# A transformer layer with a sparse-column FFN: the FFN's columns moved three groups behind the attention's front, and a new order of the prologue

## What is computed

```python
xn = layernorm(x)                                  # no gain or bias
x = x + attention(xn) + ffn(xn)

# attention: 16 heads of 16, rotary q and k, a bias by bucket of distance, causal softmax, output projection
# ffn, for each token:
similarity = l2norm(xn) @ l2norm(col_emb).T        # 16 columns
gate_values = sigmoid(gelu(xn @ gate_w1 + gate_b1) @ gate_w2 + gate_b2)
logits = similarity + gate_values
mask = one_hot(argmax(logits)); weights = mask * softmax(logits)
cols = gelu(einsum('bsd,cdn->bscn', xn, W_cols) + b_cols) * weights[..., None]   # 16 columns x 64 neurons
y = cols.reshape(B, S, -1) @ proj_w + proj_b + xn
out = (y - mean(y)) * rsqrt(var(y) + 1e-5) * ln_g + ln_b
```

## Time and profile before

| | us |
|---|---|
| three runs, median (lowest to highest) | 2100.35 (2096.41 to 2103.63) |
| the profiled execution | 2098.83 |
| its span, first to last instruction | 2097.0 |
| PE, DVE, ACT, POOL busy | 1872.3, 1595.2, 1104.2, 631.1 |

### The profile page before, as it was taken

How to read it: one execution, slowest core, us unless ns; L and a number is a source line. 1 busy time by engine, 2 the same in 40 slices (tenths; PEclk the granted TensorE clock), 3 DMA queues, 4 the chain that set the end, 5 groups by cost and what they waited for, 6 DMA issues and landing times.

```text
span 2097.0 us, 40927 instructions
## 1 busy us (share of the span) xinstructions
PE 1872.3 (89%) x10854; PEld 1023.3 (49%) x10854; DVE 1595.2 (76%) x5475; ACT 1104.2 (53%) x2142; POOL 631.1 (30%) x848
## 2 busy tenths in 40 slices
PE   4887899999999999999999999999999999997776
PEld 2654455555445555455555554455545554453223
DVE  2235788888888788887888788887887788877883
ACT  2232455555665455565555556655555556554444
POOL 4463332233333223333333133333222333300000
PEclk9989999999999999999999999999999999998988
DMA  8413122233212222232122332122222321122101
...
DMA packets 199392, 144.67 MB, mean 69 GB/s; under 512 B 60428, under 2 KB 186780, under 8 KB 199149
## 3 DMA queue, kind: packets, MB, share of 16 engines
...
## 4 chain that ended last, share of the span: by engine, by line
PE 58%; DVE 14%; issue 12%; POOL 6%; ACT 4%; SPq 4%; DMA 1%; DVEq 0%; ACTq 0%; POOLq 0%
PE scores L1079 12%; PE rows L1023 9%; PE o_bank L1007 9%; PE scores L990 7%; PE bank L1090 7%; PE bank L1036 5%; DVE rows L1172 3%; DVE scores L1151 3%; PE bank L1108 3%; ACT probs L876 3%; PE scores L1081 3%; DVE maxima L1177 2%; SPq L601 2%; POOL rot L795 1%; POOL qk L788 1%
## 5 line engine op out<-in xcount | busy, mean ns | idle before, releaser
L876 ACT ACTIVATE probs<-scores 128x512 f32<-128x512 f32 (+1 forms) x1280 | 670.4, 555 | 497.5 <-DVE scores L1151 251.2
L1177 DVE TENSOR_REDUCE maxima<-rows 128x1 f32<-128x384 f32 (+4 forms) x896 | 473.8, 551 | 120.6 <-PE rows L1023 118.5
L990 PE MATMUL scores<-stack_q,stack_k 99*128 99x512 bf16 (+3 forms) x1536 | 432.9, 337 | 96.6 <-ACT probs L876 67.8
L1023 PE MATMUL rows<-stack_k,stack_q 96*128 96x256 bf16 (+3 forms) x2048 | 460.0, 292 | 44.2 <-issue 14.8
L1172 DVE CUSTOM_DVE_ANT_0 rows<-rows,near_rows 128x256 f32<-128x256 f32 (+1 forms) x1024 | 395.2, 431 | 87.3 <-PE rows L1023 85.3
L1151 DVE TENSOR_TENSOR scores<-scores,near_cols 128x256 f32<-128x256 f32 x768 | 323.2, 433 | 68.0 <-PE scores L990 66.4
L1023 PEld LDWEIGHTS rows<-stack_k,stack_q 96*128 96x128 bf16 x2048 | 170.8, 98 | 408.8 <-issue 146.7
L1007 PE MATMUL o_bank<-probs,v_aug 128*32 128x512 f32 (+3 forms) x3072 | 322.8, 508 | 6.1 <-ACT probs L876 6.1
L1079 PE MATMUL scores<-xn_t,w_cols 128*128 128x256 f32 x1024 | 288.1, 405 | 3.1 <-ACT others_t L922 3.1
L1090 PE MATMUL bank<-w_proj,act_t 128*128 128x256 f32 x1024 | 259.2, 389 | 11.4 <-DVE y L1207 9.7
L990 PEld LDWEIGHTS scores<-stack_q,stack_k 99*128 99x128 bf16 x1536 | 144.7, 99 | 227.9 <-ACT probs L876 146.4
...
## 6 DMA issues: line engine op xcount, KB each, us to landing
...
```

The source lines that it names most:

```text
L876: act.activation(probs[:, (g * NS + s) % PROBS, h, 0:width], ring[(rings + ring_n[1]) % RING][:, 0:width], ACT.Exp, scale=float(D) ** -0.5 ...
L990: ins = pe.matmul(ring[(rings + ring_n[1]) % RING][:, c0:c0 + w], stack_k[g % 2][:, h, kb * P:(kb + 1) * P], stack_q[g % 2][:, h, q0:q0 + ...
L1023: ins = pe.matmul(tile[:, at:at + k1 - k0], stack_q[ag % 2][0:STACK, h, qb * P:(qb + 1) * P], stack_k[ag % 2][0:STACK, h, k0:k1], start=Tr ...
L1177: ins = dve.tensor_reduce(maxima[:, part, m:m + n], tile[:, at:at + n * w].rearrange("p (n w) -> p n w", w=w), AX.X, ALU.max)
```

## The change

The FFN of a chunk moves three groups later. Group G still does the front of chunk G + 5, but the neurons of chunk G + 2 and the columns of chunk G + 1. As xn and xn_t do not live that long, they are kept in one tile (`kept`), written to DRAM at `x_turn`, and read back into another (`again`, whose halves are `skip` and `ffn_t`) at the new stage `ffn_in`, at score slot 8. The first chunk writes into `again` directly. `weight` and `others_t` get a place for each of four chunks. `rest` is made from a second load of x at the new stage `rest_in` (slot 24), and stored at the new stage `keep_rest` (slot 19); x of the chunk after next is loaded at `x_turn` in place of `mask_turn`. The load of v becomes a stage of its own, `load_v`.

The prologue is no longer one chunk after the other: BETWEEN holds the second half of one front and the first half of the next. Two chunks get neurons, one gets columns. The stack halves of groups 0 and 1 are loaded as soon as two chunks are through, the 12 early row tiles stand beside the fronts of chunks 3 and 4, the 28 late ones in the last plan. POOL's rotary writes its first two products into `rot` in place of `swapped`. The near tables are loaded after the parts of the second chunk and no longer after the first chunk's v.

```diff
@@ -129,16 +129,18 @@
           6: [('columns', 7)],
           7: [('x_turn', None)],
           9: [('y2_stats', None)],
+          8: [('ffn_in', None)],
           10: [('skip', None)],
           11: [('qk_begun', 0), ('qk', 0)],
           12: [('load_q', None), ('v', 0)],
           15: [('finish', None), ('qk_begun', 1)],
           16: [('qk', 1)],
           17: [('hidden', None)],
-          19: [('v', 1)],
+          19: [('keep_rest', None), ('v', 1)],
           21: [('gate', None), ('o_turn', 0)],
           23: [('qk_turn', 0), ('choose', None)],
           25: [('left', 0), ('tie', None), ('middle', 0)],
+          24: [('rest_in', None)],
...
-ALONE = ([("stats", None), ("center", None), ("x_turn", None)] + [("columns", k) for k in range(C_PIECES)]
-         + [("qk_begun", 0), ("qk", 0), ("qk_begun", 1), ("qk", 1), ("y2_stats", None), ("skip", None),
-            ("hidden", None), ("v", 0), ("gate", None), ("v", 1), ("choose", None), ("qk_turn", 0),
-            ("left", 0), ("tie", None), ("choice", None), ("finish", None), ("middle", 0), ("qk_turn", 1),
-            ("left", 1), ("mask_turn", None)]
-         + [("neurons", (k, m)) for k in range(2) for m in range(N_PIECES)] + [("middle", 1)]
-         + [("neurons", (k, m)) for k in range(2, 4) for m in range(N_PIECES)])
-CLOSING = [("load", None), ("neurons", (0, 0)), ("neurons", (0, 1)), ("pv", NS - 1), ("o_out", 1),
+NEURONS = [("neurons", (k, m)) for k in range(EM // N_PIECES) for m in range(N_PIECES)]
+
+
+FIRST = ["stats", "center", "x_turn", "qk_begun 0", "qk 0", "qk_begun 1", "qk 1", "v 0", "v 1", "hidden", "gate"]
+BETWEEN = ["next center", "choose", "next x_turn", "qk_turn 0", "left 0", "middle 0", "later stats", "tie",
+           "next qk_begun 0", "next qk 0", "qk_turn 1", "left 1", "choice", "middle 1", "next qk_begun 1", "next qk 1",
+           "mask_turn", "next v 0", "next v 1", "next hidden", "next gate"]
+FINAL = [stage for stage in BETWEEN if stage.split()[0] not in ("next", "later")]
+CLOSING = [("load", None), ("load_v", None), ("neurons", (0, 0)), ("neurons", (0, 1)), ("pv", NS - 1), ("o_out", 1),
            ("neurons", (1, 0)), ("neurons", (1, 1)), ("neurons", (2, 0)), ("shift", None),
            ("neurons", (2, 1)), ("neurons", (3, 0)), ("neurons", (3, 1)), ("o_turn", 1), ("shift_turn", None)]
 FRONT = {"stats", "center", "x_turn", "qk_begun", "qk", "v", "hidden", "gate", "choose", "tie", "choice",
-         "qk_turn", "mask_turn", "left", "middle", "neurons", "skip"}
-FRONT_LATER = {"columns", "y2_stats", "finish"}
+         "qk_turn", "mask_turn", "left", "middle"}
+FFN = {"ffn_in", "skip", "rest_in", "neurons"}
+FFN_LATER = {"columns", "y2_stats", "finish", "keep_rest"}
...
@@ -232,7 +236,8 @@
     o = Order()
     for g in range(NG):
         has_front = batch + (g + LEAD) // NC < B
-        has_later = batch + (g + LEAD - 1) // NC < B
+        has_ffn = batch + (g + 2) // NC < B
+        has_later = batch + (g + 1) // NC < B
         has_next = not (batch == B - 1 and g == NG - 1)
         has_load = batch < B - 1 or g + 2 < NG
...
-    for g in range(-LEAD, 0):
-        plan = [p for p in ALONE if p[0] in FRONT or g > -LEAD]
-        if g == -1:
-
-            o.add("load_q", -2)
-            o.add("load_k", -2)
-            o.add("load", -2)
-            plan = with_rows(plan, len(plan) // 5, len(plan) - 1, ALL_ROWS)
-        for stage, arg in plan:
-            o.add(stage, g, arg)
-    o.add("widen", -1)
-    o.add("load_q", -1)
-    o.add("load_k", -1)
-    o.add("load", -1)
+
+    def add(stage, g):
+        stage, *arg = stage.removeprefix("next ").removeprefix("later ").split()
+        o.add(stage, g, int(arg[0]) if arg else None)
+
+    def between(g, beside):
+        for stage in BETWEEN:
+            at = g + {"next": 1, "later": 2}.get(stage.split()[0], 0)
+            if at < 0:
+                add(stage, at)
+            for stage, at, arg in beside.get(stage, []):
+                o.add(stage, at, arg)
+
+    for stage in FIRST:
+        add(stage, -LEAD)
+        if stage == "x_turn":
+            o.add("stats", -4)
+    between(-5, {})
+    between(-4, {"middle 1": [("load_q", -2, None), ("load_k", -2, None)],
+                 "next hidden": [("skip", -2, None)]})
+    pieces = [[(stage, -2, arg) for stage, arg in NEURONS[k:k + N_PIECES]] for k in range(0, len(NEURONS), N_PIECES)]
+    between(-3, {**dict(zip(("next x_turn", "next qk 0", "next qk 1", "next v 1"), pieces)),
+                 "middle 1": [("load_q", -1, None), ("load_k", -1, None)], "next gate": [("rest_in", -2, None)]})
+    early = len(EARLY) * GH
+    rows = [[("row", -1, row) for row in ALL_ROWS[k:k + 2]] for k in range(0, early, 2)]
+    between(-2, {**dict(zip(("choose", "left 0", "middle 0", "next qk 1", "next v 1", "next gate"), rows)),
+                 "middle 1": [("load", -2, None), ("load_v", -2, None)]})
+    plan = [(stage, int(arg[0]) if arg else None) for stage, *arg in map(str.split, FINAL)]
+    plan += [("y2_stats", None), ("ffn_in", None), ("load", None), ("widen", None), ("finish", None)]
+    plan += [("skip", None), ("load_v", None), ("keep_rest", None), ("rest_in", None)] + NEURONS
+    for stage, arg in [("columns", k) for k in range(C_PIECES)]:
+        o.add(stage, -1, arg)
+    done = early
+    for at, (stage, arg) in enumerate(plan):
+        o.add(stage, -1, arg)
+        upto = early + (len(ALL_ROWS) - early) * (at + 1) // len(plan)
+        for row in ALL_ROWS[done:upto]:
+            o.add("row", -1, row)
+        done = upto
     o.add("shift", -1)
     o.add("shift_turn", -1)
...
-        skip = sb("skip", [P, CT, C])
+        kept = sb("kept", [P, 2, CT * C])
+        xn = kept[:, 0, :].rearrange("p (t f) -> p t f", f=C)
+        xn_t = kept[:, 1, :].rearrange("p (k n) -> p k n", n=CH)
+        again = sb("again", [P, 2, CT * C])
+        skip = again[:, 0, :].rearrange("p (t f) -> p t f", f=C)
+        ffn_t = again[:, 1, :].rearrange("p (k n) -> p k n", n=CH)
+
+        def normed(g):
+
+            return (skip, ffn_t) if g == -LEAD else (xn, xn_t)
+
         rest = sb("rest", [P, CT, C])
         qk = sb("qk", [P, CT, 2 * C])
-        swapped = sb("swapped", [P, 2 * C])
         rot = sb("rot", [P, CT, 2 * C])
         parts = [sb(f"part{i}", [P, 2 * KC, CH], BF16) for i in range(3)]
         left = sb("left", [P, 2 * KC, P])
...
 
+        def ffn_of(b, g, ahead):
+
+            m = g + ahead
+            if g < 0:
+                return m // NC, m % NC, m
+            fb, c = b + m // NC, m % NC
+            return fb, c, fb * NC + c
+
         def next_group(b, g):
 
             ab, ag = (0, 0) if g < 0 else (b, g + 1) if g + 1 < NG else (b + 1, 0)
...
+
+                    elif stage == "load_v":
+                        tb, tg, ti = loaded_group(b, g)
+                        sp.wait_ge(v_out, (tb + 1) * (NC * 16))
+                        alone(sp)
 
                         wait(sp, v_aug_ready, ti)
                         alone(sp)
@@ -647,11 +692,11 @@
                         sp.wait_ge(v_ready, n * CT + CT)
                         alone(sp)
                         sp.dma_start(v_d[fb, :, c * CT:(c + 1) * CT, :], v[:, :, :]).then_inc(v_out, 16)
+                    elif stage == "x_turn":
                         if g > -LEAD:
-                            store_rest(fb, c, n)
-                        else:
-                            load_near()
-                    elif stage == "mask_turn":
+                            sp.wait_ge(bank_drained[i], use + 2)
+                            alone(sp)
+                            sp.dma_start(kept_d[fb, c], kept[:, :, :]).then_inc(kept_out, 16)
                         if not isinstance(n, int) or n + 2 < B * NC:
                             load_x(*((fb, c + 2) if c + 2 < NC else (fb + 1, c + 2 - NC)))
                     elif stage == "middle" and arg == 1:
@@ -660,8 +705,26 @@
                             alone(sp)
                             sp.dma_start(parts_d[fb, i, :, :, c * CH:(c + 1) * CH].rearrange("q p t -> p q t"),
                                          parts[i][:, :, :]).then_inc(parts_out[i], 16)
-                    elif stage == "finish" and isinstance(n, int) and n == B * NC:
-                        store_rest(fb, c, n)
+                        if g == 1 - LEAD:
+                            load_near()
+                    elif stage == "ffn_in":
+                        mb, mc, m = ffn_of(b, g, 2)
+                        sp.wait_ge(kept_out, m * 16)
+                        alone(sp)
+
+                        wait(sp, moments2_ready, m)
+                        alone(sp)
+                        sp.dma_start(again[:, :, :], kept_d[mb, mc]).then_inc(kept_in, 16)
+                    elif stage == "rest_in":
+                        mb, mc, m = ffn_of(b, g, 2)
+                        wait(sp, rest_out, m * 16)
+                        alone(sp)
```

(37 more changed lines are left out.)

99 lines of the change are left out of this document (52 added, 47 removed).

## The result

| | before | after |
|---|---|---|
| median, us, of the executions (their number; lowest to highest) | 2099.88 of 4 (2096.41 to 2103.63) | 2069.53 of 4 (2062.47 to 2077.07) |
| ratio, 95% interval | | 0.9852 [0.9818, 0.9886] |
| profiled execution / its span, us | 2098.83 / 2097.0 | 2062.47 / 2060.7 |
| first shift transfer issued, us | 220.8 | 167.3 |
| groups 0 to 26, us | 1628.8 | 1629.0 |

The changed kernel is faster by 1.5%, 30 us between the medians; 49 were forecast. The last three lines cut each span at SP's issues of the shift transfers, as the prediction did. The profiled execution is the fastest of the four of after, so its 36.3 us less of span is the favourable end: 53.5 us from the prologue, 3.2 from group 0 (62.0 to 58.8), 3.4 lost in groups 1 to 26, 17.0 lost in the last five.

A forecast was written before the change was run, and what follows sets the result against it. Middle groups were taken as bound by PE, the last groups by no full engine, with 224.5 us before the first score. 2098.8 - 56 (prologue) + 0 (middle) + 8 (last groups) = 2050.8, said as 2050; 8-in-10 range 2024 to 2082.

The forecast's parts named there:

- Prologue, -56: Start to first score: 168.4 us against 224.5 before, bounds 155 (-69) and 185 (-39).
- round 0: Prologue: DVE stops until the third chunk's x arrives at 53.5 us, then POOL goes on, ending at 65.
- Round 3: Prologue: POOL first held by `rest_in`'s x, then 13.5 us of POOL or 17 of DVE; end at 120, bounds 112 and 126.
- The second halves: Prologue: group 0's second stack halves landed after chunk 3's parts, taken as 128 us, from 115 to 131.
- x at 53.5: Prologue, round 0: third chunk's x, issued at about 30 us behind sheared bias writes that land at 52.7.
- Step 8: Prologue's end: shift, turn, copy 2.3 us plus 3.6 to first score, 5.9; group 1's 12 loads no longer in the way.
- bound by its chains: Prologue rival: interleaving brings little beyond the FFN that left; first score at 185 to 195, 2067 to 2077 us; 17%.
- rule against interleaving: Prologue: second engine blocked until the first's instruction ends; 7.8 us a chunk in place of 2.4, 27 us longer, 2077.
- The clock: Prologue rival: lower clock slows PE's fronts; rounds 0 and 1 together 10 us more, 2060; counted inside the forecast, no own chance.
- Middle groups, 0 with bounds of -3 and +10: 27 middle groups: reload shifts POOL 3 us inside 7 us of slack, so cost 0, bounds -3 and +10 us.
- Last groups, +8: Groups 27 to 30: 52 us of moved PE work mostly fills 47 us of idle; +8 us, bounds 0 and +20.
- give all back: Last groups rival: 52 us of PE work unhidden, 2095 us, no measurable change; 7%.

The follow-up runs named there:

- b1_x_first: Third chunk's x issued ahead of the sheared bias writes, else as the changed kernel: median 2058.15 us, ratio 0.9807 to the kernel before, first shift at 159.6.
- a2_late: Changed kernel with early stack halves and early row tiles undone, fronts still interleaved: median 2069.4 us, 0.9852 of the kernel before, first shift at 169.3.
- a3_serial_late: Changed kernel with interleaving, early stack halves and early row tiles undone: median 2079.32 us, 0.9914 of the kernel before, first shift at 180.8.
- b3_both: Changed kernel with third chunk's x ahead of the sheared writes and first `rest_in` two chunks sooner: median 2057.37 us, 0.9789 of the kernel before.
- c2_tail: Changed kernel with most FFN matmuls left out of the last groups, other work kept: median 2055.85 us, 0.9801 of before; groups 27-31 255.7 us.

## Why the prediction was right or wrong

The sign and the size of the larger term were right, the size of the smaller was not: 2050 was forecast and 2069.5 measured, inside the range, 3.5 us above the forecast's own span of 2038 to 2066; the profiled execution, 2062.5, lies inside that too.

- **Prologue, -56: right.** First score at 171.5 (168.4 forecast, 224.5 before): -53. *The steps:* round 0 with x at 54.4 (53.5) and its end at 66.6 (65); round 1's rotary at 82.9 (81); round 2 at 102.4 (103). *Round 3* was the one mis-sized: it ended at 127.1 instead of 120, above its bound of 126, since `rest_in` held POOL not a few us but 10.6. The second halves let the first late tile go at 134.8 (128 forecast), and the late tiles ended at 165.2, after 30.4 us instead of 34.5, so part of it came back.
- **A step that was right by its number and thin in its reason**: x at 53.5. I took it as queued behind the sheared writes' landing; the timeline has SP itself spending 12.2 us on the issue, and b1_x_first shows that place alone is worth 8 us.
- **Step 8, no row of loads ahead of the shift: true, and worth at most 1.7 us**, since a2_late undoes the early tiles with it. I gave the absence of the loads no term of its own, but counted it among what shortens the end. a2_late has the row back, and it is hidden. What shortened the end was that 20.2 us of FFN a chunk were gone: -40 of -53.5 is there in a3_serial_late.
- **Rival "bound by its chains"** (first score at 185 to 195): wrong in size, since interleaving bought 10 to 11.5 us. But chains there are: two late x alone cost 12.6 us (167.6 to 155.0 in b3_both).
- **The rule against interleaving** (the Trainium skill, "SBUF — State Buffer", "Who interferes with whom"): the trace agrees with it, and my reading of the 0.61 us as a price in its place was wrong. Three of DVE's rows, and POOL's beside the first two:

```profile
680.46 1.27 POOL L859 TENSOR_TENSOR qk<-qk,rotary 128x512 f32<-128x512 f32 x1
680.54 1.24 DVE L1327 SCALAR_TENSOR_TENSOR logits<-gate_th,like 128x32 f32<-128x32 f32 x1
...
1044.34 1.27 POOL L859 TENSOR_TENSOR qk<-qk,rotary 128x512 f32<-128x512 f32 x1
1044.96 0.69 DVE L1327 SCALAR_TENSOR_TENSOR logits<-gate_th,like 128x32 f32<-128x32 f32 x1
...
1047.26 0.18 DVE L1334 TENSOR_TENSOR tied<-logits,top 128x32 f32<-128x32 f32 x1
```

DVE's operation ends 0.05 us after POOL's instruction (at 1.24 us where it began 0.08 us behind its start, at 0.69 where 0.62 behind), and so do, within 0.01 us, all 49 of `logits`, `tied`, `below`, `ranked` and `others` that took over 0.24 us in before and after. What is paid is the rest of POOL's instruction. `left`, which has one of its two inputs in PSUM, took 0.68 to 0.69 us in all 64 cases in after, beside POOL or not. The price stayed low because few of them met one: before the first shift 8 of 25 did in after, for 4.0 us in all, where I had 2.4 a chunk and the rule at its full price 7.8; one chunk after the other it had been 15 of 25, for 7.8 us in all. Rounds 1 and 2 ended within 2 us of a sum without it.
- **The clock** in the rounds: it fell as feared, 0.63 in 54 to 65, and 0.78 in the last plan, which I had at full clock; both are inside the times above.
- **Middle groups, 0 with bounds of -3 and +10: inside them, some 5 us worse.** The slack after the reload is 3.3 us where I had 7 less 3, and the second wait of POOL, for the x of `rest_in`, is 1.9 us in the quoted group. Both are hidden. What isn't hidden is the clock's stretches, one to seven more of them; I had no term for those, because the profile of before, with its 9, gave me no reason to count them. Their link to the change is likely, not shown. A rival was not tested: in the groups none of the 135 small DVE operations above met a POOL instruction in before, and 26 did in after, for 13.9 us in all, mostly `logits`, in group 14 some 7 us ahead of the stretch in which DVE is full.
- **Last groups, +8: the step that failed; +17.0** in the profiled execution, and 14 to 18 more than the mean of three profiles of before in the eight others that keep these groups whole. The +8 is the sum of the four groups' upper ends (0.8 + 2.3 + 3.2 + 1.5): 52.8, 52.7, 50.5 and 49.0 us, where 53.4, 55.5, 53.1 and 50.2 were measured. Group 31, for which I had no term, grew by 2.0 more. What was wrong in it:
  - *PE's share of a front.* I took 10 us, and a middle group without it as 48.0. The subtraction that gave the 10 takes 27 for the attention, but the lines of scores, rows and `pv` make 38.0 in a middle group; durations of matmuls overlap in the pipeline, and all lines together make 68.6 where PE is busy 54.5. By difference of two rows, the middle's 54.25 less group 29's 47.45, where the front is gone and the FFN is still whole, it is 6.8. Group 29's clock was 0.97, which can hide up to 1.6 us more (an estimate: 0.03 of 53.1 us), so 6.8 to 8.4. The floor of such a group was 50 to 51 us and not 48.
  - *The projections* in 27 and 28, counted as 2: by difference to group 29 they are 2.6 us of PE in group 27 (50.05 less 47.45, clock 1.00) and 5.1 in group 28 (52.53), where the same number of matmuls met a clock of 0.94. Group 28 took 2.1 us more than group 27, with a stretch of lower clock in it. These two are PE's half, of which c2_tail gives back 8.7.
  - *Only PE was priced*, in groups where DVE is nearly as full. The FFN brings DVE's `y`, statistics and norms along; in group 30 DVE has 41.3 us, before 38.3, PE only 39.5 in 50.2, and c2_tail, with most of PE's moved work away, leaves the group at 50.0. How much of the other 8.3 us is DVE's and how much the lower clock's isn't settled.
  - *The clock, in the other direction*: in groups 27 to 30 it rose from 0.93, 0.87, 0.89 and 0.83 to 1.00, 0.94, 0.97 and 0.92, for which the sum has no term. These rows give 47 us at the lower level before and 18 after, so the same PE work was some 12 to 15 us shorter (an estimate), and 52 us of moved matmuls raised PE's busy time by only 39.5.
- **Rival "give all back"** (+52): wrong. PE's busy time in groups 27 to 30 rose from 150.0 to 189.6, by 39.5, and the groups grew by 15.0: 24.5 of it went into holes.

With the last groups at the forecast's +8 instead of +17 the profiled execution would have been at 2053.5, close to the 2050. The median of the four lies another 7 above it: the profiled one has the shortest middle, 1629.0, of the ten.
